# One VectorE operation for both one-hots of an edge column, and three tiles of gate products moved behind the recurrence

## The reference

```
x = x + relu(A_norm @ (xn @ W) + b) + linear_attention(xn)     # A_norm: edge counts and self loops, scaled by degrees
h = layernorm(x)
rw, sel  = top 2 of softmax(h @ Wgate) over 4 experts
q, k, v  = l2norm(silu(h @ Wq)), l2norm(silu(h @ Wk)), silu(h @ Wv)
per expert, a scan over the nodes:  S = S * exp(g);  S = S + k (beta (v - k S));  o = q S
core = sum over the experts of rw * o
gate = silu(h @ Wg)
x = x + (core * rsqrt(mean(core^2) + 1e-5) * o_norm_weight * gate) @ Wo
```

## Time and profile before

| | us |
|---|---|
| median of 3 runs | 1015.61 (1013.1 to 1015.81) |
| the profiled execution: its own time | 1018.47 |
| its span, first to last instruction | 1016.7 |
| TensorE busy (89% of the span) | 909.4 |
| VectorE busy (59%) | 600.5 |
| ScalarE busy (25%) | 254.0 |
| GpSimd busy (36%) | 370.0 |
| L1428, 160 operations of 180 elements | 56.1 busy, 350 ns each |
| L1430, 160 operations of 180 elements | 50.2 busy, 314 ns each |

### The profile page before, as it was taken

The page is one execution under the profiler, slowest core; times in us unless marked ns, Lnnn a source line. Parts: engine busy times, 40 slices in busy tenths (PEclk is TensorE's granted clock), DMA queues, the critical chain, the costliest instruction groups (busy, mean ns, idle before and its releaser), DMA issues.

```text
span 1016.7 us, 28629 instructions
## 1 busy us (share of the span) xinstructions
PE 909.4 (89%) x12622; PEld 583.9 (57%) x12622; DVE 600.5 (59%) x1297; ACT 254.0 (25%) x500; POOL 370.0 (36%) x303
## 2 busy tenths in 40 slices
PE   3999999988999999999999978889988889798288
PEld 2444444444666444444444458888888788788243
DVE  7799999457888323315545265546555556454274
ACT  1221122010222000023111324333433334343141
POOL 5111100000111300000788557555656464643482
PEclk9999999978999999999999989999999999999789
DMA  8400000000000140000046644434343444321452
GB/s 241 141 0 1 1 1 0 1 0 1 1 1 2 51 178 1 0 1 1 15 176 224 256 140 112 125 97 128 98 127 97 110 112 111 106 69 25 107 152 71
DMA packets 73189, 78.25 MB, mean 77 GB/s; under 512 B 34189, under 2 KB 55847, under 8 KB 73063
## 3 DMA queue, kind: packets, MB, share of 16 engines
q1 hardware_dynamic: 67943, 55.24, 19.4%
q0 software_dynamic: 5120, 21.14, 5.8%
HBM read 51.95 MB, written 24.35 MB: 75 GB/s over the span
## 4 chain that ended last, share of the span: by engine, by line
PE 80%; DVE 9%; issue 6%; POOL 3%; ACT 1%; DMA 1%; SPq 0%; DVEq 0%; POOLq 0%
PE bank L827 16%; PE bank L750 14%; PE bank L759 8%; PE bank L517 7%; PE bank L547 4%; PE bank L533 3%; PE bank L928 2%; PE bank L600 2%; DVE rows L1573 2%; POOL big L1358 2%; PE bank L839 2%; PE bank L904 2%; PE bank L524 2%; PE bank L938 2%; PE bank L942 2%
## 5 line engine op out<-in xcount | busy, mean ns | idle before, releaser
L750 PE MATMUL bank<-W,xT 128*128 128x512 f32 x320 | 138.6, 593 | 0.0
L750 PEld LDWEIGHTS bank<-W,xT 128*128 128x128 f32 x320 | 60.6, 190 | 75.7 <-issue 75.5
L759 PE MATMUL bank<-hs,big 125*125 125x512 f32 x200 | 86.6, 593 | 0.0
L1240 POOL TENSOR_TENSOR big<-big,ident_sb 125x125 f32<-125x125 f32 x10 | 11.4, 1141 | 195.8 <-ACT big L1059 195.8
L517 PE MATMUL bank<-W,xT 128*125 128x512 f32 x160 | 78.6, 610 | 0.0
L827 PE MATMUL bank<-big 64*64 64x64 f32 x1920 | 71.3, 221 | 3.4 <-issue 2.3
L1301 POOL TENSOR_TENSOR tB<-tA,masks_sb 128x512 f16<-128x512 f16 x20 | 39.4, 1968 | 94.0 <-DVE tA L1797 94.0
L827 PE MATMUL bank<-tB 64*64 64x64 f16 x2560 | 61.4, 196 | 11.3 <-issue 6.4
L827 PEld LDWEIGHTS bank<-big 64*64 64x64 f32 x1920 | 64.1, 136 | 4.8 <-issue 3.8
L533 PEld LDWEIGHTS bank<-rows 128*126 128x126 f16 x360 | 44.5, 138 | 35.6 <-issue 24.2
L759 PEld LDWEIGHTS bank<-hs,big 125*125 125x125 f32 x200 | 37.3, 188 | 47.7 <-issue 47.4
(11 more groups left out here) (287 smaller groups left out, 1910.4 us busy)
## 6 DMA issues: line engine op xcount, KB each, us to landing
big<-qkv_slots SPq DMA_DIRECT2D x40, 256.0 KB, 3.8
rows<-step_rows SPq DMA_DIRECT2D x40, 128.0 KB, 3.2
rows<-gam_rows SPq DMA_DIRECT2D x40, 128.0 KB, 3.1
big<-qkv_slots SPq DMA_DIRECT2D x80, 64.0 KB, 2.7
big<-qkv_slots SPq DMA_DIRECT2D x40, 128.0 KB, 2.9
o_slots<-big SPq DMA_DIRECT2D x40, 128.0 KB, 2.6
x_all<-in_x SPq DMA_DIRECT2D x10, 224.0 KB
out<-tC SPq DMA_DIRECT2D x10, 224.0 KB
```

What stands on the lines that cost most here:

```text
L750: last = mm(bank[:, b0, :], xT[:, k, t * P:t * P + 128], W[:, w, k, :], start=(k == 0), stop=(k == KC - 1))
L759: last = mm(bank[0:P, t % 2, :], cnt[:, s, t * P:(t + 1) * P], hs[:, s, :], start=(s == 0), stop=(s == NT - 1))
```

## The change

Three things change.

1. In `sort_four`, one `scalar_tensor_tensor` of 2 x 180 elements makes both column one-hots. The scalar of each partition is `e_col`, and `e_src` and `e_dst` come as a tensor, broadcast over 180 places each. The number of semaphore steps stays the same. The second loop over rounds (L1592 to L1595) keeps two operations; it doesn't run with these inputs.
2. The gate products of tiles 7, 8 and 9 (`LATE = 7`) move behind the recurrence on TensorE, their silus behind it on ScalarE, and their `gate_rows` into the closing loop on VectorE, one after each of the first three pairs. TensorE's wait before the recurrence is for the silus up to tile 6 alone.
3. What they read must outlive the recurrence. So `AT` and `TF` get other places, and ScalarE copies two of the four blocks of `xT` for tiles 7 to 9 (128x375 each) into `kvbd` and `iota`, ahead of the recurrence.

```diff
+LATE = 7
-        AT = [unit(xTu, 6 + s) for s in range(2)]
+        AT = [unit(big, 21), xTu[:, 3 * (N + 3) + 1:3 * (N + 3) + 1 + D].rearrange("p (a n) -> p a n", n=CL)]
-        TF = [[unit(Wu, 12 + 2 * p + s) for s in range(2)] for p in range(2)]
+        TF = [[unit(big, 8 + 11 * p + s) for s in range(2)] for p in range(2)]
+        lateT = [kvbd[:, :, :].rearrange("p c n -> p (c n)"), iota[:, :].bitcast(f32)] + [xT[:, k, LATE * P:N] for k in (2, 3)]
 # TensorE, before the recurrence
-            for t in range(2, NT):
+            for t in range(2, LATE):
                 project_rows(t, 3)
-            pe.wait_ge(S["f_act"], 4 * NT)
+            pe.wait_ge(S["f_act"], feature_count(LATE - 1, 3))
 # TensorE, behind it
+            for t in range(LATE, NT):
+                for k in range(KC):
+                    last = mm(bank[0:P, 1 + t - LATE, :], lateT[k][:, (t - LATE) * P:(t - LATE + 1) * P], W[:, 3, k, :], start=(k == 0), stop=(k == KC - 1))
+                last.then_inc(S["f_psum"], 1)
 # ScalarE, before and behind
-            for t in range(2, NT):
+            for t in range(2, LATE):
                 feature_rows(t, 3)
+            for k in range(2):
+                A(lateT[k][:, 0:N - LATE * P], xT[:, k, LATE * P:N], ACT.Copy)
...
+            for t in range(LATE, NT):
+                act.wait_ge(S["f_psum"], feature_count(t, 3))
+                A(hs[:, t, :].rearrange("p (b j e) -> p b j e", b=2, e=DH), by_halves(1 + t - LATE, P), ACT.Silu).then_inc(S["f_act"], 1)
 # VectorE, sort_four
-                    V.tensor_scalar(oh_col[:, i % (SR * SB), 0, :], iota[0:P, 0:SW], e_col[:, i:i + 1],
-                                    e_src[:, i:i + 1], ALU.is_equal, ALU.mult)
-                    V.tensor_scalar(oh_col[:, i % (SR * SB), 1, :], iota[0:P, 0:SW], e_col[:, i:i + 1],
-                                    e_dst[:, i:i + 1], ALU.is_equal, ALU.mult).then_inc(S["sort_oh"], 1)
+                    V.scalar_tensor_tensor(oh_col[:, i % (SR * SB), :, :], bm(iota[0:P, 0:SW], 2), e_col[:, i:i + 1],
+                                           e_all[:, 2:4, i:i + 1].broadcast_to([P, 2, SW]), ALU.is_equal, ALU.mult).then_inc(S["sort_oh"], 1)
 # VectorE, before the recurrence and in the closing loop
-            for t in range(NT):
+            for t in range(LATE):
                 gate_rows(t)
...
                 if g:
                     last_sum(dve, V, 2 * g - 1)
+                if g < NT - LATE:
+                    gate_rows(LATE + g)
```

## The result

The changed kernel takes 1022.57 us, median of 20 runs, against 1016.36 us for the kernel before in 20 runs beside them. The ratio is 1.0053, with a 95% interval of 1.0034 to 1.0071: 5.4 us slower (3.5 to 7.2). The forecast was 1014.2 us, the range ended at 1019.0, and "slower" had a chance of 0.13. Single runs of either kernel scatter by 2.6 to 2.8 us (standard deviation), so a single profile is read here by the length of its stages and not by its total. The profile after is of an execution of 1023.54 us, with a span of 1021.7.

The account below looks back on a forecast made before the run. TensorE was taken as the bound, with VectorE close behind in the sort. From the profiled 1018.47, + 0.6 (one-hots) - 2.0 (recurrence start) = 1017.1; the same -1.4 from the median 1015.61 gave 1014.2 us, range 1009.8 to 1019.0.

Parts of the forecast that it names:

- slower: Whole kernel: the outcome of a measurably longer time, with a difference of 0.3% or 3.0 us counted as none; chance 0.13.
- The one-hot's own rate: Sort, VectorE: the merged operation takes 0.51 us per column, 0.04 more than the two it replaces.
- This stall of 0.95 us to go: Sort, VectorE: the 0.95 us hold beside GpSimd's sum of keys vanishes with the merged operation.
- my last rival: Sort: VectorE becomes the bound from 0.53 us per column; at 0.56 it costs 8.2, giving 1021.8 us; chance 0.13.
- +0.6: Sort: merged one-hots add 0.6 us, in the query stretch and one later group; tiles 5 to 9 hide theirs.
- what speaks against the change: Sort, VectorE: joining two tensor_scalar gives up four elements per cycle for an operation of the kind limited to two.
- Start of the recurrence: Before the recurrence: features(0) waits for the load and starts 3.5 us earlier; half clock costs 2.3, leaving 1.2 us.
- 0.8 us "given back": Early recurrence: the clock returns somewhat earlier, recovering 0.8 us, a third of the 2.7 us price of the half-clock stretch.
- The rest of the recurrence shifts as it is: Recurrence after its start: no change in length; AT and TF in other places cost nothing.
- The late products were to give 2.0 us: Gate products of three tiles moved behind the recurrence: net gain 2.0 us at its start, bounds +6.2 and -1.6.
- Behind the recurrence: After the recurrence: late products fit TensorE's idle 20.97 us, ending at 959.3; silus and gate rows cost 0.
- +0.6 - 2.0 + 0: Whole kernel: one-hots cost 0.6 us, the earlier recurrence gains 2.0, and work behind the recurrence costs 0.

Follow-up runs that it names:

- e4: Kernel before with the merged one-hots, and GpSimd's sum of keys cut to 8 of 512 columns from tile 4 on; ratio 1.0034.
- e1: Kernel before with the merged one-hot edit in sort_four only; 1021.83 us against 1016.78, ratio 1.0047.
- e11: The whole changed kernel with only tile 9's gate products late instead of three tiles'; 1013.98 us against 1016.46, ratio 0.9976.
- e8: Kernel before with the merged one-hot only from group 20 on, the 80 columns of the query stretch; 1021.61 us against 1018.39, ratio 1.0042.
- e2: Changed kernel with the two old one-hot operations put back, three tiles still late; 1017.13 us against 1016.78, ratio 1.0023.
- e3: Kernel before with the new places of AT and TF and nothing else; 1016.33 us against 1016.78, ratio 1.0011.
- e5: e2 plus twelve padding matmuls of 320 columns before the recurrence; 1017.29 us against 1018.39 for the kernel before, ratio 0.9989.
- e6: e2 plus twelve padding matmuls of 16 columns before the recurrence; 1018.25 us against 1018.39 for the kernel before, ratio 0.9985.
- e9: e7 plus four padding matmuls of 16 columns before the recurrence; 1015.24 us against 1016.46 for the kernel before, ratio 0.9980.
- e7: e2 with one late tile (tile 9) instead of three; 1011.70 us against 1018.39 for the kernel before, ratio 0.9937.
- e10: e2 with two late tiles (8 and 9) instead of three; 1013.33 us against 1016.46 for the kernel before, ratio 0.9957.
- e13: e2 plus eight padding matmuls of 16 columns before the recurrence; ratio 0.9962 to the kernel before.
- e14: e2 plus four padding matmuls of 16 columns before the recurrence; ratio 1.0001 to the kernel before.
- e12: Kernel before plus eight padding matmuls of 16 columns before the recurrence; 1019.38 us against 1016.46, ratio 1.0026.

## Why the prediction was wrong

**The one-hot's own rate: right.** The new operation starts every 0.505 us (2.02 for four); I had taken 0.51.

**"This stall of 0.95 us to go": the step that failed.** I argued from L1426, which has two tensor inputs and isn't stretched next to GpSimd's sum, to a `scalar_tensor_tensor` with two tensor inputs. The new row is 3.03 us for four instead of 2.02: the new operation is held for 1.0 us, as L1428 was in the earlier trace rows.

The argument misread L1426. All six that lie next to a sum start 0.16 us ahead of it, so none of them was ever held up by one; the operation that starts while the sum runs is the next one. And the trace of before had a row of a `tensor_tensor` that starts inside a GpSimd operation: the second of the gate rows, which takes 1.64 us there instead of 0.69. The first line below belongs to the sum at 79.68 in the earlier trace rows.

```profile
79.52 0.68 DVE L1426 TENSOR_TENSOR rows<-iota_sb,gbp 125x512 f16<-125x512 f16 x1
...
584.49 1.63 POOL L1288 TENSOR_TENSOR rows<-xn,masks_sb 128x512 f32<-128x512 f32 x1 [9.76 <-DVE xn L1786]
585.03 1.64 DVE L1766 TENSOR_TENSOR hs<-hs,onorm 125x512 f32<-125x512 f32 x1
```

The tile is then 4 x (0.60 + 2.02) + 0.61 + 1.0 = 12.09 us, and 12.09 is what the trace shows. With the same sum, my own numbers would have given 4 x (0.60 + 2.04) + 0.6 + 0.95 = 12.1 against TensorE's 11.48, and the bound of my last rival, which I had put at 0.53 us per column, would have stood at 0.47 for tiles with a sum. The old kernel was exactly there: 4 x (0.60 + 4 x 0.47) + 0.6 + 0.95 is 11.5. e4, with the sum cut short, shows it in the trace; its timed runs don't confirm it.

**What it cost.** In tiles 5 to 9 and in the query stretch the trace shows 2.1 and 1.0 us, 3.1 together (116.7 or 116.8 us in after, e1 and e11, against 113.6), where I had +0.6. The mechanism is the last rival's, VectorE as the bound of the sort, though by a remaining stall and not by a slower rate; its price of 8.2 us was too high, since the query stretch gave 1.0 and not 7.2. The timed cost, 4.8 (1.9 to 7.5), holds the 3.1. That e4 and e8 cost about 4 us in the timed runs while their profiles, of executions 5 us faster than the medians, show nearly nothing stays open. So the stall is shown for the 3.1 us of the trace, and not for the whole of the timed cost.

The Trainium skill, "VectorE: DVE Perf Modes" (The perf-mode tier table), was cited for what speaks against the change, that joining two `tensor_scalar` gives up a rate of four elements per cycle. The trace doesn't bear that out as the reason: 0.505 us per column against 0.47 is a loss of 7%, and alone it was hidden in tiles 5 to 9 (e4). For the start of an operation behind its predecessor the prediction took only half of what this page of the Trainium skill says (The DRAIN you can't avoid): it adds that a next operation which isn't held starts earlier. The 0.235 us between starts in the earlier trace rows agree with that.

**Start of the recurrence: mechanism right, size a little off.** `features(0)` waits for the load, as said. Last aggregation to `features(0)` became 2.6 us shorter in after and 3.3 in e2, against 3.5. From `features(0)` to VectorE's step of unit 2 it took 29.8 us in after and 29.5 in e2 where it had been 27.5: the half clock cost 2.3 and 2.0 us, against 2.3. The net was -0.3 and -1.3, where I had -1.2 at that point. The 0.8 us "given back" later can't be separated from what follows.

**"The rest of the recurrence shifts as it is": not borne out, and the cause is open.** The late products were to give 2.0 us. Alone they cost 2.3 in the timed runs (-0.1 to +4.8), and the start of the recurrence, which still gains 0.3 to 1.3, doesn't account for that.

In the profiles, units 2 to 19 took 294.1 us on average in the five kernels with all products in their old place and no padding (before, e1, e3, e4, e8; 292.9 to 296.2), and 297.9 in the seven with two or three late tiles (295.8 to 302.1); 298.2 in after. They took 290.2 and 289.2 in the two with one late tile and no padding. The longer units go with more pauses for "issue", 45.2 us in after against 36.4. But that the kernels differ so isn't shown. The profiled executions of the five lie 1.6 us below the medians of their kernels on average, those of the seven 2.1 above, and this difference of 3.7 is as large as the 3.8 in the units. In the timed runs the six of the seven that have the old one-hots are 1.4 us faster than before on average (ratios 0.9957 to 1.0023), not slower.

Where the pauses fall does follow the number of matmuls ahead. In the kernel before, long ones recur from one group of units to the next on L858 and L904. They are on the same two statements in after and e2, which have twelve matmuls fewer there, and in e5, e6 and e9, which have as many as before. In e7, e10, e11, e13 and e14 (four or eight fewer) and in e12 (eight more) L858 has no long ones, L904 none over 0.8 us, and L928 has long ones instead. TensorE's waits from 590 to 950 us in e9 (L862 is L858 of before) and in e7 (L930 is L928 of before):

```profile
PE bank L862 <- issue: 6.1, 4, 1.9
...
PE bank L930 <- issue: 4.7, 5, 1.4
```

What they add up to doesn't follow from this: 36.4 to 45.6 us in the first set, 35.1 to 41.5 in the second.

The places of `AT` and `TF` show no cost (e3). That the position of the program matters for the time is what e9, e12 and e13 point to: four tiny matmuls took 4.4 us back (0.8 to 8.0) while they made the first step 1.7 us shorter (3.1 against 4.8), eight ahead of e2 gave 6.2 (2.7 to 9.7), and e12 shows a small loss. That a count of them explains the rest is not: e14 and e6 went against it. I carry it as open: moving instructions in front of this loop seems to be worth several microseconds either way, and I can't say ahead which way. In the prediction this should have been a term of its own, of 0 with bounds of -4 to +4, and the range should have been wider by it.

**Behind the recurrence: right.** The late products end at 962.7, in the idle time ahead of the last transposes, and these still start 21.1 us after the recurrence's last product (21.2 before). From the first of them to TensorE's last matmul it is 43.4 us against 42.5, inside the 42.2 to 43.5 of all kernels. To the end of the span it is 48.6 against 46.6, the longest of all profiles, but e4, with no late product, has 48.5. The granted clock is part of it: in the 5 us that start 1.8 us behind the first of these transposes it was 0.61 in after (974.97 to 979.97) and 0.88 in before (971.83 to 976.83).

**How the whole adds up.** +3.1 in the sort, -0.3 at the start, +3.9 in units 2 to 19 (298.2 less 294.3) are +6.7 in the profiles. The two spans differ by 5.0, since in after the time ahead of tile 5 is 3.5 us shorter, the time between the sort and the last aggregation 1.1 shorter, and all behind unit 19 2.9 longer; one profile of each can't tell these from scatter. Measured were +5.4, and +4.8 and +2.3 for the two halves. My sum was +0.6 - 2.0 + 0.

## What to carry to other kernels

Where two engines are balanced to 1%, count the stalls of the second one into its sum. A stall beside another engine's work stays until a row shows the new operation free of it. Such a row must be of an operation that starts while the other engine's runs; one that starts just ahead of it shows nothing. Move only as much work as the next wait can use: here one tile of three reached the load already (146.0 us instead of 147.9, against 145.3 with three). And where the profile shows long waits for "issue" in a loop that holds the bound, any edit ahead of that loop may carry an unknown of several tenths of a per cent, so time two or three sizes of it before you keep or drop it. Here one tile gave -0.6% and three +0.2%. And before a stage of one profile is set against a timed difference, see how far that execution lies from its kernel's median.

## What the runs showed of the hardware that I had not expected

- A VectorE operation that starts while GpSimd's addition of 512 f32 columns runs is held. A `scalar_tensor_tensor` of 360 elements in f16 loses 1.0 us (3.03 for four instead of 2.02), and a `tensor_scalar` of 180 takes 1.27 us instead of 0.32. A `tensor_tensor` of 512 in f32, which starts 0.54 us into another such GpSimd operation, takes 1.64 instead of 0.69. The `tensor_tensor` of 512 in f16 that starts 0.16 us ahead of the addition takes its 0.68 us.
- Busy matmuls don't hold the clock if a pause follows them: in e5 TensorE was busy for 7.81 of 8 us, and then 2.31 us of idleness led to 0.50, as 8.46 us of idleness did in after. With 0.45 us of idleness in e9 and 1.32 in e11 it stayed at 1.00. The Trainium skill, "TensorE: Matmul & The Clock Gate" (Loop structure matters more than you think), warns of long waits for a DMA; the traces agree.
- The half clock at the start of the recurrence goes with 1.2 to 2.3 us more up to unit 2 in the kernels without padding (28.7 us in e7 to 29.8 in after, against 27.5 in before and 27.4 in e11 at full clock). With padding it is 28.4 to 29.8 at half clock and 28.1 to 28.2 at full clock (e9, e12), so not all of it is the clock. Between the first matmuls the loop waits for other engines, as for 0.69 us on ScalarE's copy in after, at half clock, and in e9, at full.
- Four matmuls of 16 columns, 0.96 us of work just ahead of the recurrence, went with 4.4 us more (e7 to e9, give or take 3.6), and eight of them in e13 with 6.2 us less than e2 (give or take 3.5).
